# Layer 0 of a four-layer convolution network: another split and order of 32 tiles among VectorE, GpSimd and ScalarE

## Chip, cores and metric

The kernel runs on one core of one Trainium2 chip. The metric is the device time of one execution in microseconds (us); lower is better. PE is TensorE, DVE is VectorE, ACT is ScalarE, POOL is GpSimd.

## The reference, cut to what matters

The network has four layers, each x = x + layer(group_norm(x)) on x of 16 x 32 x 128 x 128 float32. The change touches layer 0 only. For each of the 16 x 32 matrices h (128 x 128, `t` counts the 32 of one image) it computes:

```python
hsum = hsum + h_t
hm = hsum / (t + 1.0)                      # running mean
Pu = hm @ Wu.T
Pv = hm @ Wv.T
pre = relu(Pu[:, :, None, :] + Pv[:, None, :, :] + b1)      # 128 x 128 x 128 values
S = sigmoid(einsum('bvud,d->bvu', pre, w2) + b2)
a_t = einsum('bvu,bud->bvd', Aa * S, h_t)
m_t = h_t * einsum('vu,bud->bvd', Am, h_t)
z_t = bet[0] * h_t + bet[1] * (a_t @ W_add.T) + bet[2] * (m_t @ W_mod.T)
```

Nearly all of the work is `pre`: for each pair (u, v) 128 sums and their ReLU, then a dot product with `w2`.

## The kernel before, in words

The program does the layers one after the other, with a barrier of all engines between its stages. `layer0` (L180) is the second stage. It works on groups of G = 4 matrices of one image, 128 groups in all, and one group is what the change calls a step. The feature index d lies on the partitions. The values `pre` of a group are made in R = 32 tiles, numbered r = 0 to 31; tile r holds four rows u (r, r + 32, r + 64, r + 96) against all v, for the four matrices: 128 partitions x 2048 values. A tile goes to slot r % 8 of the buffer `mx` (QB = 8 slots). So tile r may be made only when the dot product of tile r - 8 is done (semaphore `dot_done`).

Who makes tile r stands in one string, `MAKERS` (L175), read by `layer0_maker` (L176). There are three ways:

- "v": VectorE makes the tile with one operation (L323). It takes max(Pv, -(Pu + b1)), with Pv read from PSUM (`p_v`); that is the ReLU less a term of Pu alone.
- "a": ScalarE makes the tile with 16 small ReLU activations (L469), one for each row and matrix, with Pu + b1 as bias.
- "g": GpSimd makes the sums (L343), and ScalarE applies the ReLU in place to the whole tile (`relu_of_sums`, L450). ScalarE does that LAG = 1 place later in its own order: the ReLU of tile r comes at place r + 1, behind all else that stands at that place.

TensorE takes the tiles strictly in the order of r (L538) and adds the dot products with `w2` to PSUM. The term that "v" tiles leave out is computed by `corrections` (L504) and given to the sigmoid as part of its bias by `copy_corrections` (L420). For this a column `own_term`, worked out from the same string, tells which rows of a group were made by VectorE.

Everything else of a group lies at fixed places among the 32 tiles, in an order written out by hand for each engine. For each of the three engines, the function `group` walks r from 0 to 31:

- ScalarE: 5 the sigmoids of the group before (L431), 13 `copy_aT` (L441), 16 `copy_z` (L445), 17 `normalise` of the next group (L404), 19 `copy_hT` (L410), 22 `copy_mT` (L437), 26 `copy_projections` (L414 to L416, the last of them writes `puN`), 28 `copy_corrections` (L420). What stands at place r comes ahead of an "a" tile r, and that ahead of the ReLU of tile r - 1.
- GpSimd: 13 `weigh_sums` (L365), 14 `finish` (L374), 22 `running_mean` of the next group (L350 to L358), 31 `modulate` (L369), each ahead of its tile r.
- TensorE: behind dot 7 `weighted_sums` (L521), behind dot 8 `mix` (L529 to L531), behind dot 16 `modulation` (L515) and `transposes` (L493) for the next group, behind dot 22 `projections` (L498, L499), behind dot 24 `corrections`.
- VectorE has nothing but its tiles.
- SyncE's queue stores a group's output when `finish` is done, and then loads the inputs of the group after next into the same buffers: the values, two norm columns and a row of the step table (L261 to L263).

So two round trips leave ScalarE and come back to it in every group. The first runs from `copy_aT` over TensorE's `mix` to `copy_z`. The second runs from `copy_z` over `finish` on GpSimd, SyncE's store and loads, to `normalise`.

The loop over the groups (`over_groups`, L282) has two groups in its body. The compiler puts two loads of ScalarE's function tables into one of the two.

Of the kernel before, what the change touches and what calls it, by code (L numbers as in the profile page):

```python
# [164 lines left out]
def rounds_of(kind):  # L165

    first = 0
    for other in KINDS[:KINDS.index(kind)]:
        first += len(bases_of(other[0])) * len(bases_of(other[1]))
    pairs = [(by, bx) for by in bases_of(kind[0]) for bx in bases_of(kind[1])]  # L170
    return [(first + n, by, bx) for n, (by, bx) in enumerate(pairs)]


ROUNDS = rounds_of(KINDS[-1])[-1][0] + 1
MAKERS = "agvvvgvvagvvvgvvagvvvgvvagvvvgvv"  # L175
def layer0_maker(r):  # L176
    return MAKERS[r]

# [2733 lines left out]
def layout(I):  # L2912
# [3 lines left out]
    one = np.eye(P, dtype=np.float32)  # L2916
    own_term = np.array([[float(layer0_maker(p % len(MAKERS)) == "v")] for p in range(P)], np.float32)

# [40 lines left out]
```

## Time and profile before

| | |
|---|---|
| runs | 20044.06, 20062.94, 20100.28 us; median 20062.94 us |
| profiled execution | 20117.95 us, its span 20116.1 us |
| granted TensorE clock, mean of the span | 0.905 of full speed |
| busy over the whole span | PE 15875.9 us (79%), DVE 14851.0 (74%), ACT 12939.8 (64%), POOL 10618.2 (53%) |
| layer 0, first to last finished group | 210.8 to 5941.2 us of the span |

The shares over the whole span are means over stages of different kinds. Layer 0 takes somewhat over a quarter of the span. All that the change touches lies there, so it must be read from that stretch alone. A granted clock of 1.00 in a row is 2.4 GHz and 0.50 is 1.2 GHz.

### The profile page before, as it was taken

How to read it: one execution, taken by the hardware profiler on the slowest of the kernel's cores; microseconds unless marked ns; L12 is line 12 of the kernel's file. 1: busy time of each engine (PE TensorE's matmuls, PEld its weight loads, DVE VectorE, ACT ScalarE, POOL GpSimd, SP SyncE). 2: the span in 40 equal slices, each digit the busy share in tenths (PEclk: the TensorE clock that was granted, in tenths of full speed). 3: DMA queues.
4: the chain of work that ended last, by engine and by line, in shares of the span. 5: the costliest groups of instructions: out<-in, count | busy, mean ns of one | idle time of the engine just before them, and what ended most of it. 6: DMA issues, size and time to landing. Idle time of an engine off the chain costs nothing. (4 is left out here: it accounts for less than half of the span.)

```text
span 20116.1 us, 420070 instructions
## 1 busy us (share of the span) xinstructions
PE 15875.9 (79%) x152440; PEld 6721.8 (33%) x152440; DVE 14851.0 (74%) x15523; ACT 12939.8 (64%) x23242; POOL 10618.2 (53%) x6726
## 2 busy tenths in 40 slices
PE   6888888888867388888888884999999947366677
PEld 2333333333323022222222221555555523122234
DVE  8999999999982488888888883565666651788722
ACT  6998898889971366666666662777787841233322
POOL 5877777777760277777777773000000030777611
PEclk9999999999988699999999997898898978688888
DMA  2000000000015300000000004111111148655533
GB/s 77 12 12 12 12 12 12 12 12 12 12 66 115 104 18 18 19 18 18 19 18 18 18 18 93 24 34 33 33 34 34 37 113 185 155 110 109 104 74 91
DMA packets 1555418, 967.24 MB, mean 48 GB/s; under 512 B 805496, under 2 KB 1374305, under 8 KB 1542889
## 3 DMA queue, kind: packets, MB, share of 16 engines
q1 hardware_dynamic: 1406040, 732.86, 16.7%
q10 hardware_dynamic: 118480, 117.04, 2.2%
q0 software_dynamic: 29696, 100.68, 1.9%
q8 instruction: 832, 13.63, 0.3%
q14 instruction: 370, 3.02, 0.0%
HBM read 734.64 MB, written 215.64 MB: 47 GB/s over the span
## 5 line engine op out<-in xcount | busy, mean ns | idle before, releaser
L323 DVE TENSOR_TENSOR l_mx<-l_p_v,l_puN 128x2048 f32<-128x2048 f32 x2560 | 5637.3, 2282 | 157.9 <-PE l_p_s L538 145.0
L538 PE MATMUL l_p_s<-l_mx,l_w2z 128*32 128x512 f32 x32768 | 3827.1, 611 | 586.2 <-ACT l_mx L450 318.4
L343 POOL TENSOR_TENSOR l_mx<-l_pv,l_puP 128x2048 f32<-128x2048 f32 x1024 | 3716.7, 3646 | 320.8 <-PE l_p_s L538 315.1
L1249 DVE TENSOR_TENSOR_SCAN l1m_hs<-l1m_da,l1m_carry,l1m_pu 128x512 f32<-128x512 f32 x2304 | 2824.0, 1267 | 113.2 <-issue 12.6
L1907 ACT ACTIVATE l1d_ab<-l1d_pt 128x1024 f32<-128x1024 f32 x2304 | 2300.1, 1025 | 711.3 <-PE l1d_pt L1661 680.9
L1298 POOL TENSOR_TENSOR l1m_hc<-l1m_hs,l1m_cs 128x1024 f32<-128x1024 f32 x1152 | 2710.8, 2353 | 9.2 <-DVE l1m_hs L1249 5.7
L469 ACT ACTIVATE l_mx<-l_pv,l_puP 128x128 f32<-128x128 f32 x8192 | 2446.8, 394 | 0.8
L1785 DVE TENSOR_SCALAR l1d_hat<-l1d_ab 128x1024 f32<-128x1024 f32 x2304 | 1623.2, 705 | 814.6 <-ACT l1d_ab L1907 503.8
L1969 POOL TENSOR_TENSOR l1d_res<-l1d_res,l1d_xr 128x512 f32<-128x512 f32 x128 | 168.7, 1319 | 3543.9 <-ACT l1d_res L1916 3543.8
L1239 DVE TENSOR_TENSOR l1m_pu<-l1m_pu,l1m_bs 128x512 f32<-128x512 f32 x2304 | 1476.8, 687 | 742.7 <-PE l1m_pu L994 742.5
L538 PEld LDWEIGHTS l_p_s<-l_mx,l_w2z 128*32 128x32 f32 x32768 | 984.1, 112 | 3027.3 <-issue 1769.6
L1165 ACT ACTIVATE l1m_da<-l1m_pr,l1m_an 128x512 f32<-128x512 f32 x2304 | 1459.2, 684 | 822.1 <-PE l1m_pr L987 758.1
L450 ACT ACTIVATE l_mx<-l_mx 128x2048 f32<-128x2048 f32 x1024 | 1954.7, 1909 | 47.3 <-POOL l_mx L343 47.0
L994 PE MATMUL l1m_pu<-l1m_dts,l1m_sl 32*128 32x512 f32 x4608 | 1420.5, 692 | 535.4 <-ACT l1m_da L1165 526.5
L1696 PE MATMUL l1d_po<-l1d_hat,l1d_ring 128*32 128x128 f32 x36864 | 1641.7, 300 | 52.1 <-DVE l1d_hat L1785 46.8
L987 PE MATMUL l1m_pr<-l1m_dts,l1m_sl 32*128 32x512 f32 x4608 | 1407.5, 689 | 2.7 <-ACT l1m_da L1165 2.7
L1678 PE MATMUL l1d_pg<-l1d_wz,l1d_im 32*128 32x288 f32 x5120 | 1272.7, 573 | 72.4 <-DVE l1d_ring L1772 27.9
L2407 PE MATMUL l3a_pc<-l3a_xs,l3a_wb 128*32 128x512 f32 x9216 | 1102.5, 638 | 243.0 <-DVE l3a_pooled L2344 216.1
L1696 PEld LDWEIGHTS l1d_po<-l1d_hat,l1d_ring 128*32 128x32 f32 x36864 | 946.3, 116 | 740.5 <-issue 629.7
L1772 DVE COPY l1d_ring<-l1d_pg 128x288 f32<-128x288 f32 x1280 | 582.9, 455 | 637.0 <-PE l1d_pg L1678 633.7
L1678 PEld LDWEIGHTS l1d_pg<-l1d_wz,l1d_im 32*128 32x128 f32 x5120 | 944.3, 408 | 228.6 <-DVE l1d_ring L1772 169.9
L1661 PE MATMUL l1d_pt<-l1d_yt,l1d_rw 32*128 32x512 bf16 x4608 | 967.8, 417 | 18.6 <-issue 17.1
(342 smaller groups left out, 23729.0 us busy)
## 6 DMA issues: line engine op xcount, KB each, us to landing
n_xt<-x_after SPq DMA_DIRECT2D x48, 2048.0 KB
l3a_xs<-x_after SPq DMA_DIRECT2D x384, 256.0 KB, 5.3
l3a_xe<-x_after SPq DMA_DIRECT2D x480, 96.0 KB, 2.1
l1m_sq<-seq SPq DMA_DIRECT2D x256, 144.0 KB
n_xt<-in_x_dram SPq DMA_DIRECT2D x16, 2048.0 KB
l_xs<-in_x_dram SPq DMA_DIRECT2D x128, 256.0 KB, 2.9
x_after<-l_ot SPq DMA_DIRECT2D x128, 256.0 KB, 2.4
l1d_xr<-x_after POOLq DMA_DIRECT2D x32, 1024.0 KB, 10.0
```

Of the source, the lines that this page charges most:

```text
L323: v.tensor_tensor(mx[:, r % QB, :, :, :], columns.unsqueeze(1).broadcast_to([P, 4, G, P]), rows.broadcast_to([P, 4, G, P]), ALU.max).then_ ...
L343: g.tensor_tensor(mx[:, r % QB, :, :, :], pv[:, u, :, :].unsqueeze(1).broadcast_to([P, 4, G, P]), rows.broadcast_to([P, 4, G, P]), ALU.add ...
L450: act.activation(tile, tile, ACT.Relu).then_inc(max_by_g, 1)
L469: ins = act.activation(mx[:, r % QB, q, t, :], pv[:, u, t, :], ACT.Relu, bias=puP[:, u, t, R * q + r:R * q + r + 1])
L538: ins = pe.matmul(p_s[R * q:R * (q + 1), 512 * u:512 * (u + 1)], w2z[:, 31 - r:63 - r], mx[:, r % QB, q, :, :].rearrange("p t v -> p (t v) ...
L1239: dve.tensor_tensor(tile, tile, bs[:, u, :], ALU.mult).then_inc(dbu_done, 1)
L1249: dve.tensor_tensor_scan(hs[:, p % 3, part, :], da[:, p % 3, part, :], pu[:, LC * bank:LC * (bank + 1)], carry[:, u, c:c + 1], ALU.mult, A ...
L1298: g.tensor_tensor(hc[:, (3 * u + p) % 6], hs[:, p % 3], cs[:, u:u + 1, :].broadcast_to([NB, 2, LC]), ALU.mult).then_inc(hc_done, 2)
L1678: pe.matmul(pg[:, 512 * half_strip:512 * half_strip + KO], im[C * g:C * (g + 1), :, col_at(g, j)], wz[C * g:C * (g + 1), u, :], start=True ...
L1696: ins = pe.matmul(po[C * g:C * (g + 1), 512 * (s % 2):512 * (s % 2) + P], ring[:, (8 * u + s + k) % RING, g, k, :], hat[:, m % 3, n % 2, P ...
L1785: v.tensor_scalar(hat[:, m % 3], ab[:, m % 2], 1.0, 1.0, ALU.min, ALU.subtract).then_inc(hat_done, 1)
L1907: act.activation(ab[:, m % 2].rearrange("p a n -> p (a n)"), pt[:, 1024 * (m % 2):1024 * (m % 2 + 1)], ACT.Abs).then_inc(abs_done, 1)
```

## The change

One string is replaced. Nine tiles are "g" instead of eight, nineteen "v" instead of twenty, and four "a" as before at the same places.

```diff
 ROUNDS = rounds_of(KINDS[-1])[-1][0] + 1
-MAKERS = "agvvvgvvagvvvgvvagvvvgvvagvvvgvv"
+MAKERS = "avgvvgvvagvvvgvvagvvgvvgavvgvvgv"
 def layer0_maker(r):
     return MAKERS[r]
```

| | "a" | "g" |
|---|---|---|
| before | 0, 8, 16, 24 | 1, 5, 9, 13, 17, 21, 25, 29 |
| after | 0, 8, 16, 24 | 2, 5, 9, 13, 17, 20, 23, 27, 30 |

The places of the other work do not move. The places of the ReLUs on ScalarE move with the "g" tiles.

## Rows read from the trace of the kernel before

**Rows 1.** Windows view, 1st to 127th finish: length; PE, PEld, DVE, ACT, POOL busy; clock; DMA.
```profile
210.80:5905.40 5694.60, 4873.41 (x39312) 1848.16 (x39308) 5549.41 (x2522) 5127.84 (x10960) 4528.37 (x2143) 0.97 0.05 12
```

**Rows 2.** Waits view of ScalarE and VectorE, same stretch: us in total, times, longest.
```profile
ACT l_h L404 <- DMA l_stp<-in_step_table_dram: 297.4, 126, 3.6
ACT l_zs L445 <- PE l_p_z L531: 175.6, 126, 2.9
ACT l_mx L450 <- POOL l_mx L343: 44.9, 99, 0.6
ACT l_pv L414 <- PE l_p_v L499: 44.8, 28, 1.6
DVE l_mx L323 <- PE l_p_s L538: 144.7, 103, 3.6
```

**Rows 3.** Groups of instructions, same stretch: busy us, mean ns of one, idle before.
```profile
L323 DVE TENSOR_TENSOR l_mx<-l_p_v,l_puN 128x2048 f32<-128x2048 f32 x2522 | 5553.6, 2282 | 145.2 <-PE l_p_s L538 144.7
...
L343 POOL TENSOR_TENSOR l_mx<-l_pv,l_puP 128x2048 f32<-128x2048 f32 x1008 | 3658.7, 3646 | 308.7 <-PE l_p_s L538 308.7
...
L450 ACT ACTIVATE l_mx<-l_mx 128x2048 f32<-128x2048 f32 x1008 | 1924.3, 1909 | 45.2 <-POOL l_mx L343 44.9
...
L374 POOL TENSOR_TENSOR l_ot<-l_zs,l_xs 128x512 f32<-128x512 f32 x127 | 163.6, 1288 | 566.9 <-ACT l_zs L445 566.9
...
L469 ACT ACT_TABLE_LOAD x62 | 79.5, 1283 | 1.1
```

**Rows 4.** Timeline of ScalarE, one group (start us, us, engine, line).
```profile
3012.44 0.60 ACT L445 ACTIVATE l_zs<-l_p_z 128x512 f32<-128x512 f32 x1 [1.23 <-PE l_p_z L531]
...
3020.10 1.09 ACT L404 ACTIVATE l_h<-l_xs,l_gn 128x256 f32<-128x256 f32 x2 [2.40 <-DMA l_stp<-in_step_table_dram]
...
3025.66 4.77 ACT L469 ACTIVATE l_mx<-l_pv,l_puP 128x128 f32<-128x128 f32 x16
3030.36 0.60 ACT L414 ACTIVATE l_pv<-l_p_v 128x512 f32<-128x512 f32 x1
...
3031.42 0.69 ACT L416 ACTIVATE l_puN<-l_p_t,l_nb 128x512 f32<-128x512 f32 x1
...
3034.66 1.92 ACT L450 ACTIVATE l_mx<-l_mx 128x2048 f32<-128x2048 f32 x1 [0.50 <-POOL l_mx L343]
3036.47 4.77 ACT L469 ACTIVATE l_mx<-l_pv,l_puP 128x128 f32<-128x128 f32 x16
...
3055.85 0.60 ACT L445 ACTIVATE l_zs<-l_p_z 128x512 f32<-128x512 f32 x1 [1.14 <-PE l_p_z L531]
```

**Rows 5.** Timeline of GpSimd, same group.
```profile
3014.53 7.24 POOL L343 TENSOR_TENSOR l_mx<-l_pv,l_puP 128x2048 f32<-128x2048 f32 x2
3023.74 0.40 POOL L350 TENSOR_TENSOR l_kept<-l_sums,l_stp 128x128 f32<-128x128 f32 x1 [1.96 <-ACT l_hT L410]
...
3027.38 7.25 POOL L343 TENSOR_TENSOR l_mx<-l_pv,l_puP 128x2048 f32<-128x2048 f32 x2
```

**Rows 6.** Timeline of TensorE, same group.
```profile
3030.25 1.92 PE L538 MATMUL l_p_s<-l_mx,l_w2z 128*32 128x512 f32 x16
3032.26 1.02 PE L504 MATMUL l_p_m<-l_nw,l_puN 128*128 128x1 f32 x8
```

**Rows 7.** Timeline of TensorE and ScalarE at the start of the layer.
```profile
146.75 1.87 PE L504 MATMUL l_p_m<-l_nw,l_puN 128*128 128x1 f32 x8 [1.84 <-ACT l_puN L416]
...
148.66 0.35 ACT L420 ACTIVATE l_cb<-l_p_m,l_b2c,l_own 128x4 f32<-128x4 f32 x1 [1.96 <-PE l_p_m L504]
148.91 4.77 ACT L469 ACTIVATE l_mx<-l_pv,l_puP 128x128 f32<-128x128 f32 x16
```

**Rows 8.** Timeline of TensorE after a pause, then windows with its granted clock.
```profile
3085.86 8.84 PE L538 MATMUL l_p_s<-l_mx,l_w2z 128*32 128x512 f32 x64 [2.45 <-ACT l_mx L469]
...
3086.00:3088.00 2.00, 2.00 (x12) 0.26 (x13) 2.00 (x2) 1.98 (x2) 0.20 (x1) 0.50 0.00 0
3100.00:3101.00 1.00, 1.00 (x6) 1.00 (x6) 1.00 (x2) 0.60 (x1) 0.00 (x0) 0.50 0.00 0
```

## The prediction

> **What bounds the kernel now.** I first cut the span at the finishes of layer 0's groups. The finishing operation ran 127 times in the stretch [rows 3], so this holds 126 periods; 5694.6 us / 126 = 45.2 us for a group [rows 1]. The reader should see there that two engines are nearly full. VectorE is busy 5549.4 / 126 = 44.0 us of the 45.2, ScalarE 5127.8 / 126 = 40.7 us, GpSimd only 4528.4 / 126 = 35.9 us. From the shares alone VectorE looks like the bound, and the change takes a tile from it.
>
> Next I read the waits [rows 2]. VectorE waits 144.7 / 126 = 1.15 us a group, for TensorE to free a slot. With its busy time that makes 45.2 us. ScalarE waits 2.36 us for the loads ahead of the normalisation, 1.39 us for the mix, 0.36 us for GpSimd's sums and 0.36 us for the projections, together 4.47 us; 40.70 + 4.47 = 45.2 us. So ScalarE is full as well, if these waits can't be used for other work. I ask of each wait whether it is slack. The two large ones, 3.75 us, occur in all 126 groups [rows 2] and are the ends of round trips that ScalarE starts itself. After the copy of z (3012.44), the normalisation starts 7.66 us later (3020.10) [rows 4]; only one "a" tile stands between, and the change leaves that so. After the copy of aT, one ReLU (that of tile 13) stands ahead of the copy of z, and that also stays. More work elsewhere on ScalarE does not shorten these waits, because the start of the trip moves with it. Therefore ScalarE's own loop is the bound, and VectorE follows closely.
>
> **The change part by part.** I count from the start of the copy of z as zero.
>
> *VectorE loses a tile.* One takes 5549.4 / 2522 = 2.20 us [rows 1]. That takes VectorE from 44.0 to 41.8 us of work. I cost this at nothing, neither gain nor loss: the cover is ScalarE's loop, which VectorE does not end.
>
> *GpSimd gets a tile.* One takes 3.65 us [rows 3], 3.62 us from start to start in a pair (7.24 / 2) [rows 5]. GpSimd goes to 39.6 us of work and has had 566.9 / 126 = 4.5 us of idle time ahead of the finish alone [rows 3]. The load by itself is covered. Where its tiles stand is not, as shown below.
>
> *ScalarE gets a ReLU of 128 x 2048.* Its duration is 1909 ns [rows 3]; queued, it costs 1.81 us from start to start (3034.66 to 3036.47) [rows 4]. This is on the path: **+1.81 us**.
>
> *Tile 23 becomes "g".* Nothing changes for ScalarE from zero until its tile 24 starts at 13.22 (3025.66) and ends at 17.92 (3030.36) [rows 4], since tile 20's ReLU merely takes the place of tile 21's. GpSimd also does two tiles between its finish and the running mean, as before. It starts the running mean at 11.30 (3023.74) and its next tile at 14.94 (3027.38) [rows 5]. That tile is now 23, done at 14.94 + 3.62 = 18.56. The ReLU of 23 stands ahead of the copies of the projections, so ScalarE waits from 17.92 to 18.6: **+0.7 us**. The ReLU ends at 20.4 and the copies start there, 2.50 us later than before.
>
> *Nothing stands any more between the copies of the projections and the copy of the corrections.* Before, the ReLU of tile 25 filled that place. The row puN starts at 20.42 + 1.06 = 21.48 (1.06 from 3030.36 to 3031.42) [rows 4]. TensorE can start dots 23 and 24 only when the ReLU of 23 is done at 20.5. Two dots take 1.92 us, the corrections 1.02 us [rows 6], so they end at 23.5. At the start of the layer ScalarE did have to wait for them, and copied 0.04 us after their end (146.75 + 1.87 to 148.66), going on after 0.25 us [rows 7]. So ScalarE continues at 23.8 and has lost some 1.6 us. Then come the ReLU of 27 (to 25.6) and that of 30. GpSimd has made 23, 27 and 30 by 14.94 + 3 x 3.62 = 25.8, so the last one starts at 25.85. Tile 0 of the next group starts at 27.65. Before, it started at 3036.47 - 3012.44 = 24.03 [rows 4]. The loss is 3.62 us: 1.81 + 0.7 for the first ReLU, and 1.1 more in the stretch from puN to tile 0 (6.17 instead of 5.05 us), because the wait for the corrections is new and the wait for the last sums (0.50 us) becomes smaller.
>
> *The other moves.* From tile 0 on, ScalarE has the same sequence as before, with the ReLU of 2 where that of 1 was. GpSimd does the modulation to 27.1 and tile 2 to 30.7, tile 5 to 34.3, tile 9 to 37.9, while ScalarE wants them at 32.3, 35.1 and 41.6. These moves cost nothing as long as that lead of 0.8 us or more holds; if it goes, each us of delay at 5 is a us on the path. "v" tiles at 1, 6, 7, 21, 22, 25, 26, 29 and 31 shift among themselves. VectorE needs slot r - 8 freed for each; where this makes it idle, it has 3.6 + 2.2 us of new room in a group. No DMA is moved and no queue is passed; the store and loads follow the finish as now.
>
> *The clock.* After a pause of 2.45 us TensorE's granted clock fell to 0.50, the 1.2 GHz level, while it took dots; it was at 0.50 again within the mix of that group [rows 8]. Mixing slowly lengthens the wait for it to as much as 2.9 us [rows 2], against 1.14 in a group at full clock [rows 4]. The mean is 1.39, so 0.25 us a group is now lost to that. In the new order TensorE pauses before the ReLU of 23 and for over 3 us before dot 0 (dots end near 28.7, tile 0 at 32.4). A bound below is no further loss, the bound above is 1.7 us for the mix in every group plus a slow pair of dots with the corrections (1.87 instead of 1.02 us [rows 6, 7], the dots perhaps 1.9 us more). I take +0.2 us, close to what is lost now, since the dots behind the pause have slack and the mix comes some 11 us later.
>
> **Sum.** 3.62 + 0.2 = 3.8 us a group, x 126 = about 480 us. The first and last groups lack part of the sequence; I leave them out, at a few us. On the profiled execution this gives 20117.95 + 480 = 20598 us. That execution is 0.27% above the median of the three runs, so I put the gain or loss on the median: 20062.94 + 480 = 20543 us. A measurement of this kernel can tell some 0.3%, 60 us, from no change.
>
> **Rivals.**
>
> *Only the work is added.* The new waits dissolve, for instance because GpSimd runs earlier and the corrections hide. Then +1.81 x 126 = +228 us, 20291 us. The least that ScalarE's loop allows is its work and two round trips, 40.70 + 1.81 + 3.75 = 46.3 us, or +1.07 x 126 = +134 us, 20197 us. For it speaks that each new wait is under 2 us; against it, that both stand in a row of operations on engines that run strictly in order. Chance 0.18, for +60 (0.3%) to +370 us.
>
> *The clock decides.* The pauses before dots 0 and 23 bring the low clock into the corrections and into most mixes. With 1.7 us in each mix and half of the upper bound at the corrections (1.4 us) in place of the 0.2 us, it is 3.62 - 0.25 + 3.1 = 6.5 us, +815 us, 20880 us; if only the mixes are slow, 5.1 us and +640 us, 20700 us. For it speaks the row after the 2.45 us pause; against it, the mean clock of 0.97 over the whole stretch [rows 1], though TensorE waits in every group already. Chance 0.18. The Trainium skill, "TensorE: Matmul & The Clock Gate", section "HAM oscillation — how this bites in real kernels", says that a loop whose bursts are separated by long enough pauses pays the cold clock anew in each turn. By that rule this rival would be the likeliest.
>
> *VectorE is the bound, and the kernel gets faster.* Then a group takes 19 x 2.20 + 1.15 = 43.0 us, 2.2 less, -280 us, 19783 us. It decides if ScalarE's waits fall from 4.47 to under 43.0 - 42.5 = 0.5 us, and there is any gain only if they fall under 45.2 - 42.5 = 2.7 us. For it speaks VectorE's 97% share of the stretch; against it, that the two round trips alone make 3.75 us. Chance 0.05. The Trainium skill, "Perfetto Trace Analysis", section "Optimizing Scalar/DVE Operations", says that with a saturated VectorE it may pay to hand work to ScalarE or even GpSimd. Taken for VectorE alone it would give this case.
>
> *No change within 60 us.* It needs ScalarE to swallow the ReLU in its waits almost exactly, chance 0.04. That the change doesn't do what it says can be left out: every engine and the correction column read the same string.
>
> **How the numbers follow.** My forecast, +370 to +620 us, has a chance of 0.55; with the rivals this is 1.0. The range leaves out faster, same and part of the lower rival below (0.05 + 0.04 + a few hundredths), and the upper half of the clock's case above. It runs from +217 us, 20280, to +697 us, 20760. Faster 0.05, within 0.3% 0.04, slower 0.91.
>
> **What would show it.** Right: a group of layer 0 at about 49 us; ScalarE busy 42.5 us a group and waiting for the corrections (L420 on TensorE, about 1.5 us, new) and for GpSimd's sums (L450, some 0.7 to 1 us); its waits for the loads and the mix nearly as before; VectorE's waits at 5 to 7 us. Wrong: a wait for the loads or the mix below 1 us, VectorE still waiting about 1 us, or the wait for the corrections missing. A clock clearly under 0.97 in the stretch with a wait for the mix near 3 us would speak for the clock.

## The result, and the profile after

| | before | after |
|---|---|---|
| median, us | 20081.6 (4 runs) | 20610.8 (4 runs) |
| profiled execution: span, us | 20116.1 | 20681.6 |
| layer 0, from the 1st to the 127th finish, us | 5694.6 | 6229.6 |
| one group, mean of these 126, us | 45.20 | 49.44 |
| the rest of the span, us | 14421.5 | 14452.0 |
| granted TensorE clock in layer 0 | 0.97 | 0.92 |

The changed kernel is slower: ratio 1.0259, 95% interval 1.0212 to 1.0307. The medians differ by 529 us; the forecast was +480 us. In the two profiled executions 535 of the 565 us stand in layer 0. The other 30 us are of the size by which the rest of the span differs between executions of any of these kernels (14388 to 14497 us in the ones below). So I compare the stretch of 126 groups wherever a few tens of us matter.

The windows view of the kernel after, for the same stretch as [rows 1] (length; PE, PEld, DVE, ACT and POOL busy; clock; DMA):

```profile
215.00:6444.60 6229.60, 5153.05 (x39316) 1888.10 (x39312) 5331.54 (x2394) 5366.18 (x11087) 4979.45 (x2268) 0.92 0.04 11
```

The groups of instructions in it, against [rows 3]:

```profile
L323 DVE TENSOR_TENSOR l_mx<-l_p_v,l_puN 128x2048 f32<-128x2048 f32 x2394 | 5332.0, 2284 | 898.3 <-PE l_p_s L538 895.6
L343 POOL TENSOR_TENSOR l_mx<-l_pv,l_puP 128x2048 f32<-128x2048 f32 x1134 | 4110.5, 3644 | 433.6 <-PE l_p_s L538 431.8
...
L450 ACT ACTIVATE l_mx<-l_mx 128x2048 f32<-128x2048 f32 x1134 | 2150.1, 1904 | 102.2 <-POOL l_mx L343 98.2
```

VectorE did get 218 us less to do (5331.5 against 5549.4) and ScalarE 238 us more. The stretch grew all the same. The waits view says how (us in total, times, longest), against [rows 2]:

```profile
DVE l_mx L323 <- PE l_p_s L538: 895.6, 627, 4.2
...
POOL l_ot L374 <- ACT l_zs L445: 518.6, 126, 6.5
...
ACT l_cb L420 <- PE l_p_m L504: 321.1, 126, 3.1
ACT l_h L404 <- DMA l_stp<-in_step_table_dram: 293.6, 126, 3.7
...
ACT l_zs L445 <- PE l_p_z L531: 142.8, 126, 2.9
...
ACT l_mx L450 <- POOL l_mx L343: 98.2, 179, 0.8
```

VectorE now waits 896 us for slots, where it waited 145 us: it is ahead, and what it gained it spends waiting. On ScalarE the accounts close. Its busy time grew by 238 us, the wait for the corrections is new with 321 us, and the wait for GpSimd's sums grew by 53 us. Three waits shrank: the projections (-45), the mix (-33) and the loads (-4). Together this is +531 us of the 535.

One undisturbed group on ScalarE (TensorE at full clock ahead of the corrections), in the timeline of the kernel after (start, length, engine, line), against [rows 4]:

```profile
2985.44 0.60 ACT L445 ACTIVATE l_zs<-l_p_z 128x512 f32<-128x512 f32 x1 [1.24 <-PE l_p_z L531]
2985.93 4.78 ACT L469 ACTIVATE l_mx<-l_pv,l_puP 128x128 f32<-128x128 f32 x16
2992.97 1.09 ACT L404 ACTIVATE l_h<-l_xs,l_gn 128x256 f32<-128x256 f32 x2 [2.26 <-DMA l_stp<-in_step_table_dram]
...
2998.52 4.78 ACT L469 ACTIVATE l_mx<-l_pv,l_puP 128x128 f32<-128x128 f32 x16
3003.89 1.91 ACT L450 ACTIVATE l_mx<-l_mx 128x2048 f32<-128x2048 f32 x1 [0.59 <-POOL l_mx L343]
...
3006.75 0.69 ACT L416 ACTIVATE l_puN<-l_p_t,l_nb 128x512 f32<-128x512 f32 x1
3008.80 0.35 ACT L420 ACTIVATE l_cb<-l_p_m,l_b2c,l_own 128x4 f32<-128x4 f32 x1 [1.36 <-PE l_p_m L504]
3009.05 3.94 ACT L450 ACTIVATE l_mx<-l_mx 128x2048 f32<-128x2048 f32 x2
3012.90 4.77 ACT L469 ACTIVATE l_mx<-l_pv,l_puP 128x128 f32<-128x128 f32 x16
...
3032.77 4.77 ACT L469 ACTIVATE l_mx<-l_pv,l_puP 128x128 f32<-128x128 f32 x16
```

And GpSimd in the same group, against [rows 5]:

```profile
2996.61 0.40 POOL L350 TENSOR_TENSOR l_kept<-l_sums,l_stp 128x128 f32<-128x128 f32 x1 [1.92 <-ACT l_hT L410]
...
3000.22 10.84 POOL L343 TENSOR_TENSOR l_mx<-l_pv,l_puP 128x2048 f32<-128x2048 f32 x3
3011.01 1.29 POOL L369 TENSOR_TENSOR l_mhT<-l_mT,l_hT 128x512 f32<-128x512 f32 x1
```

The reader can follow the new chain. The running mean starts at 2996.61. The first of three tiles in a row starts at 3000.22 and is done 3.61 us later (10.84 / 3). ScalarE is free 0.59 us earlier and waits for it (3003.89). The copies of the projections come behind. Then nothing is left to do until TensorE has the corrections: 1.36 us of idle time ahead of 3008.80. Two ReLUs follow back to back (3009.05, 3.94 us for both), since the last sums are ready at 3000.22 + 10.84 = 3011.06, just behind the end of the first.

### The profile page after: what moved, and what is told of

Its sections match the earlier page's. It is cut to its first block and busy times, and to the rows that moved or that the text cites. A ratio compares the mean times of both kernels' runs of the same rounds, so it can differ in the third digit from the quotient of the medians.

```text
span 20681.6 us, 420326 instructions
## 1 busy us (share of the span) xinstructions
PE 16190.8 (78%) x152440; PEld 6776.8 (33%) x152440; DVE 14638.3 (71%) x15395; ACT 13183.0 (64%) x23370; POOL 11070.5 (54%) x6854
## 5 line engine op out<-in xcount | busy, mean ns | idle before, releaser
L323 DVE TENSOR_TENSOR l_mx<-l_p_v,l_puN 128x2048 f32<-128x2048 f32 x2432 | 5416.0, 2284 | 916.2 <-PE l_p_s L538 901.0
L538 PE MATMUL l_p_s<-l_mx,l_w2z 128*32 128x512 f32 x32768 | 4129.0, 652 | 891.7 <-ACT l_mx L450 524.5
L343 POOL TENSOR_TENSOR l_mx<-l_pv,l_puP 128x2048 f32<-128x2048 f32 x1152 | 4175.7, 3644 | 447.3 <-PE l_p_s L538 439.7
L450 ACT ACTIVATE l_mx<-l_mx 128x2048 f32<-128x2048 f32 x1152 | 2184.2, 1904 | 107.0 <-POOL l_mx L343 102.7
L538 PEld LDWEIGHTS l_p_s<-l_mx,l_w2z 128*32 128x32 f32 x32768 | 1031.2, 117 | 3517.4 <-issue 1949.4
```

Source lines behind the costliest of these rows:

```text
L323: v.tensor_tensor(mx[:, r % QB, :, :, :], columns.unsqueeze(1).broadcast_to([P, 4, G, P]), rows.broadcast_to([P, 4, G, P]), ALU.max).then_ ...
L343: g.tensor_tensor(mx[:, r % QB, :, :, :], pv[:, u, :, :].unsqueeze(1).broadcast_to([P, 4, G, P]), rows.broadcast_to([P, 4, G, P]), ALU.add ...
L450: act.activation(tile, tile, ACT.Relu).then_inc(max_by_g, 1)
L538: ins = pe.matmul(p_s[R * q:R * (q + 1), 512 * u:512 * (u + 1)], w2z[:, 31 - r:63 - r], mx[:, r % QB, q, :, :].rearrange("p t v -> p (t v) ...
```

## The experiments

For each, "stretch" is the time from the first to the 127th finish of layer 0 in the profiled execution. The two medians of group times are for the group without and the group with the two table loads. Before they were 43.3 and 46.1 us, after 48.1 and 50.9 us. Each ratio is to executions of the kernel before taken beside that run; their medians were 20063, 20089 and 20133 us.

| kernel | ratio to before, 95% interval | stretch, us | group medians, us | clock |
|---|---|---|---|---|
| before | | 5694.6 | 43.3, 46.1 | 0.97 |
| after | 1.0259 (1.0212 to 1.0307) | 6229.6 | 48.1, 50.9 | 0.92 |
| after, again | 1.0246 (1.0216 to 1.0276) | 6228.7 | 48.1, 50.9 | 0.92 |
| new places, 8 g tiles | 1.0074 (1.0050 to 1.0098) | 5794.8 | 44.0, 47.3 | 0.95 |
| old places, 9 g tiles | 1.0238 (1.0177 to 1.0298) | 6107.7 | 46.8, 49.6 | 0.97 |
| the same, tile 27 short | 1.0090 (1.0057 to 1.0124) | 5899.2 | 45.1, 47.9 | 0.96 |
| after, corrections copied later | 1.0236 (1.0184 to 1.0289) | 6128.8 | 46.8, 49.6 | 0.94 |
| after, TensorE's pause filled | 1.0300 (1.0235 to 1.0365), then 1.0243 (1.0208 to 1.0278) | 6131.7, then 6133.3 | 46.8, 49.8 | 0.96 |
| after, VectorE halved | 1.0281 (1.0241 to 1.0320) | 6229.0 | 48.1, 50.9 | 0.92 |
| before, VectorE halved | 0.9997 (0.9975 to 1.0019) | 5677.7 | 43.3, 46.1 | 0.97 |
| after, loads earlier | 1.0180 (1.0126 to 1.0233) | 6012.1 | 46.3, 49.1 | 0.92 |
| before, loads earlier | 0.9933 (0.9914 to 0.9952) | 5536.9 | 43.3, 44.6 | 1.00 |

### Which half of the change costs: the places or the count

The new places with tile 23 given back to VectorE:

```diff
-MAKERS = "avgvvgvvagvvvgvvagvvgvvgavvgvvgv"
+MAKERS = "avgvvgvvagvvvgvvagvvgvvvavvgvvgv"
```

> The changed kernel with tile 23 given back to VectorE: the new places, but the old counts (8 g, 20 v). Theory (ScalarE's loop is the bound; each added ReLU costs 1.8 us a group and each wait at a fixed place its own length): without the ReLU of 23 and the wait for its sums the copies of the projections start at 17.9 again; the wait for the corrections stays (about 1.4 us), the rest follows, and tile 0 starts near 24.7 instead of 24.0, so 0.6 us a group more than before in a group at full clock. With something for the clock: +60 to +200 us against the kernel before, 20140 to 20280 us. Rival (the spread itself is what costs, because VectorE waits for slots behind other tiles): it stays near the changed kernel, above +350 us. Second rival (the spread costs nothing): within 60 us of the kernel before.

The median was 20210 us against 20063 us of the kernel before, +148 us. The windows row and two of its waits:

```profile
211.50:6006.30 5794.80, 4977.74 (x39312) 1876.61 (x39308) 5555.56 (x2521) 5126.74 (x10960) 4527.30 (x2143) 0.95 0.05 12
```

```profile
ACT l_cb L420 <- PE l_p_m L504: 152.0, 126, 1.2
...
ACT l_mx L450 <- POOL l_mx L343: 12.9, 26, 0.7
```

The stretch is 100 us longer than before, 0.8 us a group, where 0.6 plus something for the clock was expected. The wait for the corrections is there with 1.2 us a group although GpSimd and ScalarE make the old number of tiles. So that wait belongs to the places alone. Both rivals fall: the difference is far under 350 us, and its interval (+100 to +197 us) lies above 60 us.

The old places with a ninth g tile:

```diff
-MAKERS = "agvvvgvvagvvvgvvagvvvgvvagvvvgvv"
+MAKERS = "agvvvgvvagvvvgvvagvvvgvvagvgvgvv"
```

> The kernel before with tile 27 made by GpSimd and ScalarE: the old places, but the new counts (9 g, 19 v). Theory: GpSimd now makes three tiles (25, 27, 29) between the running mean and tile 0, the last of them is done 25.8 us after the copy of z, and its ReLU ends at 27.65 instead of 24.0, as in the changed kernel. So +3.6 us a group, +450 us against the kernel before, though the wait for the corrections is filled by the ReLU of 25; no pause of TensorE ahead of the corrections, so no clock loss beyond that of before. +400 to +480 us. Rival (only ScalarE's added 1.8 us of work counts): +230 us. Rival (VectorE is the bound): faster than the kernel before by some 100 to 280 us.

The median was 20536 us, +473 us; the stretch grew by 413 us.

```profile
213.40:6321.10 6107.70, 4951.28 (x39316) 1826.12 (x39312) 5298.55 (x2394) 5368.45 (x11087) 4977.60 (x2268) 0.97 0.04 11
```

```profile
ACT l_mx L450 <- POOL l_mx L343: 256.4, 250, 1.7
```

The clock is at 0.97 as before, and no wait for the corrections is left, yet a group takes 46.8 us as a full-clock group of the changed kernel does. The wait for GpSimd's sums is 256 us instead of 45. So the ninth g tile costs most of the 535 us at either set of places: 413 us at the old ones, 435 us (6229.6 - 5794.8) at the new ones. VectorE's relief brings nothing back: it waits 807 us. The forecast of +400 to +480 us held.

### The added work and the added lateness

The last kernel again, with GpSimd writing only half of tile 27; half of that tile's sums are left out:

```diff
+                        nq = 2 if r == 27 else 4
-                        g.tensor_tensor(mx[:, r % QB, :, :, :], ...
+                        g.tensor_tensor(mx[:, r % QB, 0:nq, :, :], ...
```

> The kernel before with tile 27 as a ninth g tile (as in old_spread_9g), but GpSimd writes only two of its four rows q, in about half the time; ScalarE's ReLU of it stays whole. Left out: half of the sums of tile 27. It parts the added work from the added lateness. Theory: GpSimd's last sums are then done at about 24.0 us instead of 25.8, ScalarE never waits for them, and only the ReLU's 1.81 us are left: groups of 45.0 and 47.9 us, +230 us against the kernel before (+170 to +260), 240 us below old_spread_9g. Rival (GpSimd's lateness is hidden, the whole +470 us is ScalarE's work and the ring): as old_spread_9g within 60 us.

It measured 20310 us against 20133 us of the kernel before on that chip, ratio 1.0090.

```profile
211.60:6110.80 5899.20, 4967.34 (x39316) 1821.98 (x39312) 5296.04 (x2394) 5354.78 (x11087) 4760.95 (x2268) 0.96 0.04 11
```

```profile
ACT l_mx L451 <- POOL l_mx L344: 76.9, 137, 0.9
```

The median is 177 us higher, where +170 to +260 us was expected. The group medians are 45.1 and 47.9 us, as forecast: the ReLU alone is 1.8 us a group. The stretch is 204.6 us above before and 208.5 us below the kernel with the whole tile. So, at the old places, half of the cost of a ninth tile is ScalarE's work. The other half is that GpSimd needs 3 x 3.6 us between the running mean and tile 0 of the next group, where ScalarE left it room for two.

### Is VectorE on the path?

In both kernels VectorE wrote only two of the four rows of each of its tiles; half of its sums and maxima are left out.

```diff
+            v.memset(mx[:].rearrange("p s q t c -> p (s q t c)"), 0.0)
-                        v.tensor_tensor(mx[:, r % QB, :, :, :], columns.unsqueeze(1).broadcast_to([P, 4, G, P]),
-                                        rows.broadcast_to([P, 4, G, P]), ALU.max).then_inc(max_by_v, 1)
+                        v.tensor_tensor(mx[:, r % QB, 0:2, :, :], columns.unsqueeze(1).broadcast_to([P, 2, G, P]),
+                                        rows[:, 0:2].broadcast_to([P, 2, G, P]), ALU.max).then_inc(max_by_v, 1)
```

> The kernel before with each tile of VectorE only half written, in the same way; left out is the same part. Theory (ScalarE's loop with its round trips is the bound before the change too, VectorE just under it): the undisturbed groups stay at 43.2 and 46.1 us, since VectorE's 44.0 us lie under their mean of 44.7; 0 to -60 us against the kernel before. Rival (VectorE is the bound before the change, as its 97% share suggests): a group falls to ScalarE's busy time plus little, 41 to 42.5 us, -340 us or more.

> The changed kernel with each tile of VectorE only half written (two of its four rows q; the other half keeps what was in the slot), so VectorE's operation takes about half the time. Left out: half of the sums and maxima of the v tiles. Theory (after the change VectorE has room and is not on the path): the same time as the changed kernel within 60 us. Rival (the new places make VectorE late, which is why its waits on TensorE grew from 145 to 896 us): faster than the changed kernel by 100 us or more.

The windows row of the kernel before with VectorE halved:

```profile
228.40:5906.10 5677.70, 4868.84 (x39312) 1842.69 (x39308) 2934.36 (x2520) 5127.78 (x10960) 4525.52 (x2143) 0.97 0.05 12
```

The windows row of the kernel after with VectorE halved:

```profile
233.00:6462.00 6229.00, 5156.68 (x39316) 1884.35 (x39312) 2823.81 (x2394) 5367.03 (x11087) 4979.65 (x2269) 0.92 0.04 11
```

VectorE's busy time falls from 5549 to 2934 us in the kernel before, and the stretch shrinks by 17 us; the ratio is 0.9997. In the kernel after it falls from 5332 to 2824 us, and the stretch changes by 0.6 us. An engine that was busy for 97% of the stretch was not the bound before the change, and still less after it. The two engines don't slow each other's tiles either, which would be another reading: one tile of GpSimd takes 3646 ns in the kernel before and 3644 after, and 3645 and 3643 with VectorE halved.

### Is ScalarE's round trip on the path?

SyncE's queue was given another order, first in the changed kernel. `load` is split into `load_values` (the values) and `load_small` (norm columns and step table row). Nothing is left out.

```diff
             with sp.Fori(0, N // 2 - 1) as j:
                 for u in range(2):
+                    sp.wait_ge(mean_ready, j * 2 + u + 1)
+                    load_small(j * 2 + u + 2, u)
+                    sp.wait_ge(out_ready, j * 2 + u + 1)
+                    load_values(j * 2 + u + 2, u)
                     store(j * 2 + u, u)
-                    load(j * 2 + u + 2, u)
```

> The changed kernel with SyncE's queue in another order: the two small loads of the group after next are issued as soon as its buffers are free (once that buffer's running mean is done), the load of the values directly behind the finish, and the store last. It shortens the round trip from the copy of z to the normalisation by three issues, about 1.7 us. Theory (ScalarE's loop with its round trips is the bound): the wait for the loads falls from 2.3 to about 0.7 us a group, and the time by about 1.5 us x 126 = -190 us against the changed kernel (-130 to -220). Rival (VectorE, GpSimd or TensorE is the bound and the wait is slack): the wait gets shorter, the time stays within 60 us.

The median was 20429 us, 181 us below the changed kernel's 20611, and the stretch 217 us shorter. The intervals of the two ratios just overlap, but the four executions (20391 to 20449 us) all lie below the ten of the changed kernel (20564 to 20684 us).

```profile
215.10:6227.20 6012.10, 5169.78 (x39316) 1927.76 (x39312) 5317.18 (x2394) 5384.34 (x11087) 4980.19 (x2268) 0.92 0.04 11
```

```profile
ACT l_hT L416 <- PE l_p_t L499: 54.6, 126, 0.5
...
ACT l_h L410 <- DMA l_xs<-in_x_dram: 0.2, 1, 0.2
```

The wait for the loads is gone (0.2 us in all, instead of 294; 0.7 us a group had been expected to stay). In its place ScalarE waits 55 us for TensorE's transposes, and its wait for the mix grew by 27 us. 2.3 us of waiting a group were cut and the time fell by 1.73 us a group, so the round trip was on the path.

The same order in the kernel before:

> The kernel before with SyncE's queue in the new order (small loads early, values directly behind the finish, store last). Theory: ScalarE's loop shortens by the 1.7 us that it did in the changed kernel, to a mean of about 43 us undisturbed; then VectorE's 44.0 us of work are the bound, at 44.1 to 44.4 us a group instead of 45.2: -100 to -140 us against the kernel before. It would be faster than both kernels. Rival (VectorE is the bound already): no change within 60 us.

It measured 19945 us against 20089 us, ratio 0.9933. It is faster than both kernels, and by 144 us slightly more than the 100 to 140 expected.

```profile
212.30:5749.20 5536.90, 4841.02 (x39312) 1711.38 (x39308) 5536.90 (x2521) 5136.07 (x10960) 4530.74 (x2142) 1.00 0.05 12
```

```profile
L329 DVE TENSOR_TENSOR l_mx<-l_p_v,l_puN 128x2048 f32<-128x2048 f32 x2521 | 5541.0, 2279 | 0.0
```

```profile
3023.62 0.60 ACT L451 ACTIVATE l_zs<-l_p_z 128x512 f32<-128x512 f32 x1 [1.23 <-PE l_p_z L537]
...
3028.80 1.08 ACT L410 ACTIVATE l_h<-l_xs,l_gn 128x256 f32<-128x256 f32 x2
```

The normalisation now starts 5.18 us after the copy of z (3023.62 to 3028.80) instead of 7.66, right behind tile 16. VectorE is busy 5536.9 of 5536.9 us and has no wait left. The mean group, 43.94 us, is 20 tiles of VectorE and nothing else. Now VectorE is the bound. Yet this change would not pay even here. The changed kernel with the same order of the queue is the run above: 6012.1 us against 5536.9, 475 us more, 3.8 us a group. There VectorE waits 685 us, while ScalarE's busy time and waits fill the stretch. Taking a tile from the bound helps only if the engines that get it have room for it.

### The clock

In the changed kernel the undisturbed group takes 46.8 us, but the median is 48.1: the undisturbed group is the exception. In 98 of the 126 groups ScalarE waited 2.7 us or more for the corrections, in the other 28 it waited 1.2 to 1.4 us. The timeline of TensorE shows dots 23 and 24 of two groups:

```profile
3052.52 1.92 PE L538 MATMUL l_p_s<-l_mx,l_w2z 128*32 128x512 f32 x16 [2.58 <-ACT l_mx L450]
...
3941.84 3.40 PE L538 MATMUL l_p_s<-l_mx,l_w2z 128*32 128x512 f32 x16 [2.58 <-ACT l_mx L450]
```

The windows view of just these two stretches (clock third from the end):

```profile
3052.50:3054.40 1.90, 1.88 (x17) 0.44 (x17) 0.93 (x2) 1.61 (x3) 1.90 (x2) 1.00 0.00 0
3941.84:3945.20 3.36, 3.36 (x17) 0.62 (x17) 1.52 (x2) 1.59 (x3) 3.36 (x2) 0.55 0.00 0
```

The copy of the corrections behind the second:

```profile
3946.27 0.35 ACT L420 ACTIVATE l_cb<-l_p_m,l_b2c,l_own 128x4 f32<-128x4 f32 x1 [2.84 <-PE l_p_m L504]
```

Both follow the same pause of 2.58 us, and in both the dots and projections ahead of the pause ran at 2.4 GHz. In the first group the dots ran at 2.4 GHz and took 1.92 us. In the second they ran mostly at 1.2 GHz (0.55 in the mean), took 3.40 us, and ScalarE's wait for the corrections was 2.84 instead of 1.36 us. Two experiments take hold of that. In the first, the copy of the corrections stands one place later, so that the ReLU of tile 27 lies ahead of it:

```diff
-            prepare = {..., 26: copy_projections, 28: copy_corrections}
+            prepare = {..., 26: copy_projections, 29: copy_corrections}
```

> The changed kernel with the copy of the corrections at place 29 of ScalarE's order instead of 28, so that the ReLU of 27 lies ahead of it and fills the wait for TensorE. Theory: at full clock nothing is gained, since ScalarE then waits the same time for the sums of tile 30 (done at 25.8). What is gained is what the low clock adds to the corrections: groups go from 48.2 and 50.8 us to 46.8 and 49.5, 1.3 us x 126 = -165 us against the changed kernel (-100 to -190). The wait L420 on L504 (318 us) nearly vanishes, the wait L450 on L343 (97 us) grows by about 150 us. Rival (the wait for the corrections lies wholly on the path): -320 us. Rival (it lies on no path, TensorE or VectorE sets the pace): no change.

```profile
214.30:6343.10 6128.80, 5037.00 (x39316) 1901.61 (x39312) 5317.72 (x2394) 5382.52 (x11087) 4981.12 (x2268) 0.94 0.04 11
```

```profile
ACT l_mx L450 <- POOL l_mx L343: 220.3, 284, 1.4
...
ACT l_cb L420 <- PE l_p_m L504: 45.2, 48, 1.1
```

The waits moved as expected (corrections 321 to 45 us, sums 98 to 220 us) and the group medians are 46.8 and 49.6 us. The stretch fell by 101 us, at the low end of the 100 to 190 expected, not by 165. The wait for the mix took 41 us back (184 instead of 143 us in all). The medians of all runs differ by only 70 us (20541 and 20611 us), with overlapping intervals. The gain is clear in the stretch of the profiled execution; in the time of the whole kernel it is not clear of noise. The wait for the corrections as a whole was not on the path, since GpSimd's sums end just behind it.

In the second, TensorE got work for its pause:

```diff
                     if following is not None and r == 22:
                         projections(i + 1, 1 - u)
+                        for _ in range(2):
+                            pe.matmul(p_a[:, :], wu[:, :], mean[:, :, :].rearrange("p t c -> p (t c)"), start=True, stop=True)
```

> The changed kernel with two more 128x128x512 matmuls behind the projections, into a PSUM bank that nothing reads then, so that TensorE has about 2 us of work in its pause of 2.6 us ahead of dot 23. Theory (the pause brings the low clock into dots 23 and 24, which take 3.4 instead of 1.9 us and so lengthen the wait for the corrections): those dots stay at 2.4 GHz, the wait L420 on L504 falls from 2.5 to about 1.4 us a group, and the groups go from 48.1 and 50.9 to 46.8 and 49.6 us: -165 us against the changed kernel (-80 to -170), though work is added. Rival (the low clock has another cause, the longer pause ahead of dot 0): the wait stays, the time stays within 60 us or rises.

```profile
214.00:6345.70 6131.70, 5191.48 (x39820) 1979.09 (x39816) 5330.88 (x2394) 5375.48 (x11087) 4978.74 (x2268) 0.96 0.04 11
```

```profile
3057.16 1.88 PE L553 MATMUL l_p_a<-l_mean,l_wu 128*128 128x512 f32 x4
3060.01 1.92 PE L538 MATMUL l_p_s<-l_mx,l_w2z 128*32 128x512 f32 x16 [0.97 <-ACT l_mx L450]
```

```profile
ACT l_cb L420 <- PE l_p_m L504: 175.6, 126, 2.1
```

In this profiled execution the dots follow at full clock, the wait for the corrections fell to 1.4 us a group (over 2 us in only 7 of the 126), and the stretch is 98 us shorter although work was added. But the four executions were 20535, 20541, 20746 and 20747 us, at mean clocks of 0.903, 0.901, 0.886 and 0.887. The profiled one was the best of them. I therefore ran it again, beside the changed kernel:

> The changed kernel itself again, beside after_pe_filled_2 on one chip, since the executions of after_pe_filled fell into two groups, 20535 to 20541 and 20746 us, with mean granted clocks of 0.90 and 0.89. Theory (the time of the changed kernel hangs on how often the low clock falls into the dots ahead of the corrections): executions of 20560 to 20690 us, the longer ones at the lower clock.

> The changed kernel with the two extra matmuls behind the projections, again. Theory: where the clock stays high they hold it, 20530 to 20550 us, -70 us or more against the changed kernel beside it; where it falls ahead of them they take 4 us at the low clock and delay dots 23 and 24, 20740 to 20750 us. So two groups of executions again, and a median that can fall in either. Rival: the two groups belong to the chip's state, not to the extra work; then after_same shows two groups as far apart.

The changed kernel gave 20589 to 20661 us at clocks of 0.894 to 0.889. The filled one gave 20511 to 20677 us at 0.905 to 0.893, median 20610 against 20626 us. The two sharp groups of executions did not come back; my expectation of them was wrong. The longer executions of one kernel are, by and large, those with the lower mean clock over the whole span. My theory put that into layer 0, and for the changed kernel the traces don't bear it out: its two profiled executions differ by 48 us, but their stretches are 6229.6 and 6228.7 us. The difference stands outside layer 0. The filled kernel's two profiled executions were among its shortest (20535 and 20544 us) and have stretches of 6131.7 and 6133.3 us. So within layer 0 the filling gave 95 to 98 us both times. No long execution of it was profiled, so it stays open where those lose up to 200 us more. Over the whole kernel the filling is inconclusive as a remedy.

## Why the prediction was right

**The bound.** Right. "ScalarE's own loop is the bound" is shown from both sides: halving VectorE's work changes nothing, and shortening ScalarE's round trip makes both kernels faster (217 us of the stretch after, 158 us before). That VectorE "follows closely" is shown too. Before the change it lay only about 1 us under, and it took over when the normalisation came 2.5 us earlier (5.18 instead of 7.66 us behind the copy of z).

**The added ReLU, +1.81 us.** Right: 1.8 us in the group medians of the kernel with the short tile 27, +205 us over the stretch, where 1.81 x 126 = 228.

**The wait for tile 23 (+0.7 us) and the missing cover of the corrections.** Right in place and size: idle for 0.59 us and 1.36 us. Tile 0 was to start 27.65 us after the copy of z; it started at 3012.90 - 2985.44 = 27.46. An undisturbed group took 46.8 us, 3.5 more than 43.3, where the sum said 3.62. The mean wait for the corrections, though, was 321.1 / 126 = 2.55 us, not the 1.5 named as a sign; the rest is the clock's. The old places with nine g tiles show that the sum does not depend on the corrections: the pace of GpSimd's three tiles gives the same 46.8 us. In the prediction this stood as the start of the ReLU of 30 at 25.85; the wait for the corrections ate what would otherwise have been a wait for these sums.

**The clock, +0.2 us.** This term was too small. Undisturbed groups would have a mean of (46.8 + 49.6) / 2 = 48.2 us; the mean was 49.44, so 1.2 us went to slow stretches, against 0.5 before (45.20 against 44.7, the mean of 43.3 and 46.1). The term is about +0.7 us, some 90 us in all, more than three times what I took. I had reasoned that "the dots behind the pause have slack". That holds for those behind the pause ahead of dot 0, but not for dots 23 and 24, behind which ScalarE stood idle for the corrections. The mean wait for the mix even fell, from 1.39 to 1.13 us, so I had feared the wrong place. The rival on the clock had priced the right place (1.4 us at the corrections; 2.55 - 1.36 = 1.2 us measured); the forecast had left it out. What kept the total near the forecast is that the clock cost less elsewhere: the waits for the mix and for the projections shrank by 78 us together. The clock of the stretch fell from 0.97 to 0.92. The Trainium skill, "TensorE: Matmul & The Clock Gate", section "HAM oscillation — how this bites in real kernels", says that long enough pauses between bursts bring the cold clock back each time. The trace agrees for most groups (98 of 126 with the long wait for the corrections) and not for all: the same pause of 2.58 us was followed by full speed in one and by half speed in another.

**The rivals.** "Only the work is added" (+228 us) is the kernel with the short tile 27, not the change. "VectorE is the bound" is excluded by the halved VectorE. The Trainium skill, "Perfetto Trace Analysis", section "Optimizing Scalar/DVE Operations", says that handing work on may pay when VectorE is saturated. Here VectorE was nearly saturated and the hand-over cost 2.6%, because ScalarE had no room for the ReLU and GpSimd's sums came late.

**Sum.** 3.5 + 0.7 = 4.2 us a group; measured were 49.44 - 45.20 = 4.24 us, x 126 = 535 us, against 3.8 us and 480 us forecast. The sum of the waits came out 0.1 us too large and the clock 0.5 us too small.

## What to carry to other kernels

A busy share of 97% does not make an engine the bound. Add each engine's waits to its busy time, and ask of each wait whether it is slack or the far end of a round trip that the engine itself started; such a wait moves along with added work and cannot absorb it. Then count what the receiver of the work must finish by which place: at the old places the ninth tile cost as much by coming late as by its own 1.8 us. Where an engine's loop contains a round trip over a DMA queue, the cheapest gain may be the order of the issues in that queue: here 0.7% without moving any work.

## What the runs showed of the hardware that had not been expected

The order of four issues in one DMA queue (values, two small loads, store) was worth 1.25 us a group in the kernel before and 1.73 us in the changed one. With it, VectorE ran 2521 operations without a wait in 5537 us, and TensorE's clock was 1.00 over the whole stretch, as it was in no other kernel here (0.92 to 0.97). TensorE's longest wait for a tile was 1.1 us there, against 2.5 us in the kernel before. That the shorter pauses kept the clock up fits this; it was not tested by itself.
